# Gathers of the experts' stage without a bounds check: 80 indirect DMAs on GpSimd's queue

## The chip, the cores and the metric

One core of one Trainium2 chip runs the whole program. The metric is the device time of one execution in microseconds (us); the time before is the median of 3 runs.

## The reference, cut to what matters

8 sequences of 1024 tokens, 128 numbers each. A Mamba-2 mixer with an MLP comes first, then a mixture of experts; both with a layer norm ahead of them, a layer norm behind them, and a residual. The part around the change is the second:

```python
probs = jax.nn.softmax(x @ Wr + br, axis=-1)
gates, ids = jax.lax.top_k(probs, K)               # N = 8192 tokens, K = 2, E = 8
...
valid = rank < cap                                 # cap = ceil(1.2 * N / E) = 1229 tokens for each expert
pos = jnp.where(valid, s_ids * cap + rank, E * cap)
disp_tok = jnp.zeros((E * cap + 1,), jnp.int32).at[pos].set(s_tok)[:E * cap]
xg = x[disp_tok].reshape(E, cap, Dm)               # the gather
h = jax.nn.silu(jnp.einsum('ecd,edh->ech', xg, W1) + b1[:, None, :])
out = jnp.einsum('ech,ehd->ecd', h, W2) + b2[:, None, :]
gated = out * disp_g.reshape(E, cap, 1)
y = jnp.zeros((N, Dm), x.dtype).at[disp_tok].add(gated.reshape(E * cap, Dm))
```

## The kernel before, in words

The program has stages that end in a barrier of all engines: norms and decays, the state-space mixer, its MLP, routing, and last the experts' stage with the final sum and norm. Routing writes a table `token_rows` of 8192 rows to HBM; a row is a token's 128 numbers and its two gates, 130 float32, 520 bytes. It also leaves two arrays of row numbers in SBUF, `token_of` and `choice_of`, each 128 x 80 uint32. Each expert has a region of 1280 slots (10 columns of 128), of which 1229 can hold a token: the last column of each expert always has 51 vacant rows or more. A vacant slot's `token_of` is clamped to a row number of the table (line 1741: max with 0), and its `choice_of` is a number beyond the 16384 rows of `choice_rows`, so that the scatter leaves that row out.

The experts' stage (lines 1745 to 2022) goes over 24 blocks `n` of 2 to 4 columns: `sizes` is (2, 4, 4) for the first expert, (4, 3, 3) for the next six, (4, 4, 2) for the last. Each block passes through these steps, each on one engine:

- `fetch(n)`, GpSimd (line 1865 on; the DMA is recorded as line 1871): one indirect DMA for each column gathers 128 rows of `token_rows` into `xg`, a ring of 8 blocks. It waits for block n - 8 to have left `xg` (`need` on `s_pt`, `s_g1`, `s_g2`).
- `turn(n)`, TensorE (line 1891): transposes into `e_pT`; it waits for the gathers of its block. VectorE copies them to `e_xgT` (line 1984) and makes the gates (lines 1975 to 1980).
- `up(n)` (line 1900), `silus(n)` on ScalarE (line 1943), `down(n)` (line 1908), `outs(n)` on ScalarE (line 1950), `back(n)` (line 1916): two matmul layers and the transpose back.
- `results(n)`, VectorE (line 1992): times the gate, into `yo`, a ring of 8 blocks.
- `leave(n)`, GpSimd (line 1875 on; the DMA is recorded as line 1879): one indirect DMA for each column scatters the rows into `choice_rows`. It waits for `results(n)`.

The order on each engine is written out by `staged([(lag, step), ...])`: at turn i it issues each step for block i - lag, in the order of the list. On GpSimd that is `staged([(0, fetch), (LAG, leave)])` with LAG = 5: fetch(0) to fetch(5) come first, then leave(0), fetch(6), leave(1) and so on, and after fetch(23) and leave(18) the last five `leave` stand alone. On TensorE it is up(i - 2), down(i - 3), back(i - 4), turn(i). So of GpSimd's 160 indirect DMAs the first 20 are gathers, then the two kinds alternate in groups of 2 to 4: 19 times a scatter follows a gather, and 18 times a gather follows a scatter.

Behind the experts, SyncE waits for the last scatters (line 1851) and loads `choice_rows` in 19 groups (lines 1854, 1855); TensorE adds the two choices (line 1931), VectorE and ScalarE do the norm (lines 2000 to 2019), SyncE stores.

With `bounds_check=TOKENS - 1` each indirect DMA of line 1871 is preceded on GpSimd's queue by a register instruction (MOVE) that puts 8191 into a register, which the DMA names as an operand; line 1879 does the same with 16383.

Of the kernel before, what the change touches and what calls it, by code (L numbers as in the profile page):

```python
# [36 lines left out]
TOKENS = SEQS * LEN  # L37
# [22 lines left out]
def need(eng, sem, t, back=0):  # L60

    value = t + 1 - back
    if not isinstance(value, int) or value > 0:
        eng.wait_ge(sem, value)
# [33 lines left out]
def build(nc, x, ln_w, ln_b, in_proj_w, conv_w, conv_b, dt_bias, A_log, D_skip, rms_w, out_proj_w,  # L98
# [4 lines left out]
    with ExitStack() as ctx:  # L103
# [9 lines left out]
        def sem(name):  # L113
            s = nc.alloc_semaphore(name=name)
            stage_sems.append(s)
            return s
# [484 lines left out]
        with ExitStack() as st:  # L601
# [45 lines left out]
            def staged(stages):  # L647

                for i in range(PAIRS + max(lag for lag, _ in stages)):
                    for lag, stage in stages:  # L650
                        if 0 <= i - lag < PAIRS:
                            stage(i - lag)
# [1092 lines left out]
        with ExitStack() as st:  # L1745
# [9 lines left out]
            RING = 8  # L1755
# [59 lines left out]
            s_xg = [sem(f"e_xg{k}") for k in range(RING)]  # L1815
# [47 lines left out]
            @block.gpsimd  # L1863
            def _(g):
                def fetch(n):
                    need(g, s_pt, n, RING)
                    need(g, s_g1, n, RING)
                    need(g, s_g2, n, RING)
                    for i in range(sizes[n]):
                        c = starts[n] + i  # L1870
                        g.indirect_dma_start(xg[:, n % RING, i, :], None, table,  # L1871
                                             bass.IndirectOffsetOnAxis(ap=token_of[:, c:c + 1], axis=0),
                                             bounds_check=TOKENS - 1, oob_is_err=False).then_inc(s_xg[n % RING], 16)

                def leave(n):
                    need(g, s_yo, n)
                    for i in range(sizes[n]):
                        c = starts[n] + i
                        g.indirect_dma_start(choice, bass.IndirectOffsetOnAxis(ap=choice_of[:, c:c + 1], axis=0),  # L1879
                                             yo[:, n % RING, i, :], None, bounds_check=2 * TOKENS - 1,  # L1880
                                             oob_is_err=False).then_inc(s_scat[n % RING], 16)
                g.wait_ge(filled, 16 * FILLS)
                staged([(0, fetch), (LAG, leave)])
# [161 lines left out]
```

## Time and profile before

| | |
|---|---|
| median of 3 runs | 878.65 us (876.77 to 880.98) |
| the profiled execution | 879.82 us; its span in the profile 878.1 us |
| TensorE's mean granted clock | 0.885 of 2.4 GHz |
| experts' stage, first gather to end of last scatter | 613.6 to 831.5 us |
| engines, share of the span busy | TensorE 81%, VectorE 69%, ScalarE 56%, GpSimd 50% |

PE is TensorE's matmuls, DVE VectorE, ACT ScalarE, POOL GpSimd, SP SyncE; POOLq and SPq are what those engines' queues issue themselves. Times of rows count from the start of the span. "issue" as a releaser means that the engine waited for nothing that the profile shows. Durations of single GpSimd instructions are given in ns.

### The profile page before, as it was taken

The numbers are of one execution on the slowest core, as the hardware profiler recorded it, in microseconds if no ns is written. First come the engines' busy times: TensorE is split into PE (matmuls) and PEld (weight loads), VectorE is DVE, ScalarE is ACT, GpSimd is POOL, SyncE is SP. The second block draws the span as 40 slices with busy tenths as digits, with TensorE's granted clock in tenths as the row PEclk, the third lists the DMA queues.
The fourth block names the chain that finished last, engine by engine and source line by source line (L and its number), as shares of the span: only waits on it lengthen the run. The fifth ranks groups of instructions, "written<-read, shape, count | busy, mean of one in ns | idle before, by whom it ended". The sixth has DMA issues, their size and how long they took to land. (4 is left out here: it accounts for less than half of the span.)

```text
span 878.1 us, 14619 instructions
## 1 busy us (share of the span) xinstructions
PE 710.7 (81%) x3872; PEld 493.1 (56%) x3872; DVE 606.9 (69%) x2161; ACT 490.8 (56%) x1207; POOL 442.8 (50%) x576
## 2 busy tenths in 40 slices
PE   7657999999999997899999721046698888888994
PEld 3425677777777775798989720023354444444442
DVE  7957999999999993799999868897111211121067
ACT  4864666676667675687877415434243432334157
POOL 7612767667667664234433350000757777777500
PEclk8867999999999999999999855555699998999998
DMA  9930000000000001500000004000322212221196
GB/s 219 388 129 14 1 1 1 2 1 1 2 1 1 1 1 34 159 1 2 3 1 1 1 0 196 0 0 2 99 64 72 74 50 74 73 75 50 41 352 219
DMA packets 50414, 52.92 MB, mean 60 GB/s; under 512 B 7576, under 2 KB 39624, under 8 KB 50080
## 3 DMA queue, kind: packets, MB, share of 16 engines
q1 hardware_dynamic: 44496, 41.62, 14.6%
q0 software_dynamic: 5120, 10.37, 4.4%
q8 instruction: 30, 0.49, 0.2%
q14 instruction: 48, 0.39, 0.1%
q10 hardware_dynamic: 720, 0.05, 0.1%
HBM read 28.04 MB, written 24.18 MB: 59 GB/s over the span
## 5 line engine op out<-in xcount | busy, mean ns | idle before, releaser
L890 DVE SCALAR_TENSOR_TENSOR s_cv<-s_pU,tap_w,s_cv 128x256 f32<-128x256 f32 x372 | 153.4, 476 | 12.4 <-ACT s_cv L821 12.0
L1871 POOL DMA_INDIRECT arena<-token_rows,token_of x80 | 81.4, 1017 | 112.3 <-issue 111.7
L1992 DVE TENSOR_TENSOR arena<-e_pB,e_gate 128x384 f32<-128x384 f32 (+2 forms) x24 | 14.5, 603 | 123.9 <-PE e_pB L1916 123.9
L1879 POOL DMA_INDIRECT choice_rows<-arena,choice_of x80 | 79.7, 996 | 32.7 <-issue 22.6
L1943 ACT ACTIVATE e_h<-e_pH,e_bcols 128x384 f32<-128x384 f32 (+2 forms) x96 | 58.7, 616 | 65.6 <-PE e_pH L1900 63.1
L1900 PE MATMUL e_pH<-e_xgT,e_w 128*128 128x384 f32 (+2 forms) x192 | 83.4, 584 | 0.0
L689 POOL TENSOR_TENSOR s_xa<-s_xt,arena 128x512 f32<-128x512 f32 x32 | 34.5, 1077 | 88.3 <-ACT s_xt L839 88.3
L821 ACT ACTIVATE s_cv<-s_pU,tap_b,tap_w 128x256 f32<-128x256 f32 x124 | 63.7, 561 | 23.4 <-PE s_pU L723 23.0
L723 PE MATMUL s_pU<-arena,w_in 128*128 128x262 f32 x248 | 69.3, 403 | 7.7 <-DVE s_cv L890 3.4
L1908 PE MATMUL e_pO<-e_h,e_w 128*128 128x384 f32 (+2 forms) x192 | 72.7, 522 | 0.4 <-ACT e_oT L1950 0.4
L1372 PE MATMUL m_pM<-w_m,m_h 128*128 128x128 f32 x512 | 62.5, 275 | 0.1
L1363 PE MATMUL m_pH<-m_hT,w_m 128*128 128x256 f32 x256 | 60.7, 380 | 2.1 <-ACT m_h L1246 1.5
L1372 PEld LDWEIGHTS m_pM<-w_m,m_h 128*128 128x128 f32 x512 | 59.7, 192 | 0.3 <-issue 0.3
L1900 PEld LDWEIGHTS e_pH<-e_xgT,e_w 128*128 128x128 f32 x192 | 40.1, 220 | 28.9 <-issue 21.2
L1908 PEld LDWEIGHTS e_pO<-e_h,e_w 128*128 128x128 f32 x192 | 36.7, 191 | 33.3 <-issue 20.6
L1207 POOL TENSOR_TENSOR arena<-arena,m_un 128x256 f32<-128x256 f32 (+1 forms) x32 | 22.5, 703 | 64.9 <-DVE m_un L1282 64.9
L723 PEld LDWEIGHTS s_pU<-arena,w_in 128*128 128x128 f32 x248 | 43.0, 197 | 17.0 <-DVE s_cv L890 7.6
L1363 PEld LDWEIGHTS m_pH<-m_hT,w_m 128*128 128x128 f32 x256 | 46.2, 190 | 7.5 <-ACT m_hT L1239 2.6
L1246 ACT ACTIVATE m_h<-m_pH,b_col 128x256 f32<-128x256 f32 x128 | 50.2, 485 | 0.0
L1984 DVE COPY e_xgT<-e_pT 128x384 f32<-128x384 f32 (+2 forms) x24 | 14.4, 599 | 48.3 <-PE e_pT L1891 48.3
L1950 ACT ACTIVATE e_oT<-e_pO,e_bcols 128x384 f32<-128x384 f32 (+2 forms) x24 | 14.8, 617 | 54.8 <-PE e_pO L1908 54.8
L701 POOL TENSOR_TENSOR s_y<-s_y,s_dx 128x512 f32<-128x512 f32 x32 | 40.9, 1277 | 4.9 <-DVE s_y L923 4.9
(305 smaller groups left out, 1874.3 us busy)
## 6 DMA issues: line engine op xcount, KB each, us to landing
choice_rows<-zrow SPq DMA_DIRECT2D x16, 512.0 KB, 7.7
arena<-choice_rows SPq DMA_DIRECT2D x28, 256.0 KB, 5.3
token_rows<-arena SPq DMA_DIRECT2D x8, 520.0 KB, 5.8
n_x<-in_L_attn_x_dram SPq DMA_DIRECT2D x8, 512.0 KB, 7.6
arena<-in_L_attn_x_dram SPq DMA_DIRECT2D x8, 512.0 KB, 4.8
e_w<-in_L_ffn_W_dram SPq DMA_DIRECT2D x16, 256.0 KB, 3.2
out_dram<-arena SPq DMA_DIRECT2D x14, 256.0 KB, 4.2
decay_rows<-arena SPq DMA_DIRECT2D x2, 1024.0 KB, 4.8
```

The costliest lines, as they stand in the source:

```text
L701: g.tensor_tensor(y2[:, :], y1[:, p % 2, :], dx[:, p % 4, :], ALU.add).then_inc(s_y2, 1)
L723: pe.matmul(pU[m % 2][:, 0:G2 * XBLK], w_in[:, P * m:P * (m + 1)], xT[:, G2 * p:G2 * (p + 1), :].rearrange("p t c -> p (t c)"), start=True ...
L821: a.activation(by_tile(cv[:, p % 2, m, :]), columns(m)[:, :, 0:P], ACT.Identity, bias=tap_b[:, m:m + 1], scale=tap_w[:, m, 0:1]).then_inc( ...
L890: v.scalar_tensor_tensor(out=by_tile(cv[:, p % 2, m, :]), in0=columns(m)[:, :, tap:tap + P], scalar=tap_w[:, m, tap:tap + 1], in1=by_tile( ...
L1246: ins = a.activation(h1[:, m % NB, c, :], pH[half_][:, N * (c % 2):N * (c % 2 + 1)], ACT.Relu, bias=b1_col[:, c:c + 1])
L1363: ins = pe.matmul(pH[half_][:, N * c:N * (c + 1)], w_m1[:, P * f:P * (f + 1)], hT[:, m % NB, :], start=True, stop=True)
L1372: ins = pe.matmul(pM[m % 2][:, P * i:P * (i + 1)], h1[:, m % NB, c, P * i:P * (i + 1)], w_m2[:, c, :], start=(c == 0), stop=(c == NF - 1))
L1871: g.indirect_dma_start(xg[:, n % RING, i, :], None, table, bass.IndirectOffsetOnAxis(ap=token_of[:, c:c + 1], axis=0), bounds_check=TOKENS ...
L1879: g.indirect_dma_start(choice, bass.IndirectOffsetOnAxis(ap=choice_of[:, c:c + 1], axis=0), yo[:, n % RING, i, :], None, bounds_check=2 * ...
L1900: pe.matmul(pH[c][:, 0:w], we1[:, expert(n) % 2, P * c:P * (c + 1)], xgT[:, n % 3, 0:w], start=True, stop=True).then_inc(s_ph, 1)
L1908: ins = pe.matmul(pO[:, 0:w], we2[:, expert(n) % 2, c, :], hb[:, n % 2, c, 0:w], start=(c == 0), stop=(c == NF - 1))
L1943: a.activation(hb[:, n % 2, c, 0:w], pH[c][:, 0:w], ACT.Silu, bias=bcols[:, f:f + 1]).then_inc(s_h, 1)
```

## The change

The keyword `bounds_check` is taken away from the gathers. The scatters of line 1879 keep theirs.

```diff
@@ fetch(n)
                         c = starts[n] + i
                         g.indirect_dma_start(xg[:, n % RING, i, :], None, table,
                                              bass.IndirectOffsetOnAxis(ap=token_of[:, c:c + 1], axis=0),
-                                             bounds_check=TOKENS - 1, oob_is_err=False).then_inc(s_xg[n % RING], 16)
+                                             oob_is_err=False).then_inc(s_xg[n % RING], 16)
```

## Rows read from the trace of the kernel before

**Rows 1.** The page: span, engines' busy time, the span in 40 slices.
```profile
span 878.1 us, 14619 instructions
...
PE 710.7 (81%) x3872; PEld 493.1 (56%) x3872; DVE 606.9 (69%) x2161; ACT 490.8 (56%) x1207; POOL 442.8 (50%) x576
...
PE   7657999999999997899999721046698888888994
...
POOL 7612767667667664234433350000757777777500
PEclk8867999999999999999999855555699998999998
```

**Rows 2.** Busy time by stretches of 26 us: time, busy (instructions), clock, DMA share, GB/s.
```profile
core 0: us, PE busy (x) PEld busy (x) DVE busy (x) ACT busy (x) POOL busy (x), PEclk, DMA share, GB/s
643.00:669.50 26.50, 26.50 (x90) 14.59 (x89) 5.70 (x20) 12.79 (x20) 19.17 (x19) 1.00 0.22 64
669.50:695.50 26.00, 20.26 (x66) 11.31 (x65) 4.52 (x15) 9.12 (x15) 19.90 (x21) 0.93 0.25 71
722.00:748.00 26.00, 21.42 (x66) 12.06 (x65) 4.47 (x15) 8.39 (x14) 19.90 (x21) 0.87 0.26 70
774.00:800.00 26.00, 19.98 (x65) 11.26 (x64) 4.68 (x15) 7.75 (x14) 19.90 (x21) 0.93 0.27 71
sum 157.00, PE 132.45 PEld 73.70 DVE 28.37 ACT 57.07 POOL 119.17; mean PE 22.07 PEld 12.28 DVE 4.73 ACT 9.51 POOL 19.86
```

**Rows 3.** Waits by engine, stretch 610 to 840: total us, times, longest us.
```profile
POOL arena L1871 <- issue: 111.7, 78, 88.2
PE e_pT L1891 <- DMA arena<-token_rows,token_of: 33.1, 15, 5.3
POOL choice_rows L1879 <- issue: 22.6, 74, 0.3
POOL choice_rows L1879 <- DVE arena L1992: 10.2, 6, 5.2
POOL arena L1871 <- DVE arena L1992: 0.6, 2, 0.3
```

**Rows 4.** GpSimd in order of time (start us, us; idle before in brackets).
```profile
613.64 1.26 POOL L1871 DMA_INDIRECT arena<-token_rows,token_of  x1 [88.18 <-issue]
615.21 1.00 POOL L1871 DMA_INDIRECT arena<-token_rows,token_of  x1 [0.31 <-issue]
...
644.84 1.03 POOL L1879 DMA_INDIRECT choice_rows<-arena,choice_of  x1 [5.16 <-DVE arena L1992]
...
790.65 1.05 POOL L1871 DMA_INDIRECT arena<-token_rows,token_of  x1 [0.30 <-issue]
792.00 1.01 POOL L1871 DMA_INDIRECT arena<-token_rows,token_of  x1 [0.30 <-issue]
793.32 1.00 POOL L1871 DMA_INDIRECT arena<-token_rows,token_of  x1 [0.30 <-issue]
794.62 1.00 POOL L1871 DMA_INDIRECT arena<-token_rows,token_of  x1 [0.30 <-issue]
795.93 1.02 POOL L1879 DMA_INDIRECT choice_rows<-arena,choice_of  x1 [0.30 <-issue]
...
801.20 1.01 POOL L1871 DMA_INDIRECT arena<-token_rows,token_of  x1 [0.30 <-issue]
```

**Rows 5.** Lines 1871 and 1879, all: duration ns min/median/max, first and last start.
```profile
L1871 POOLq MOVE  x80: 29/29/29, 612.7 to 790.2; - x80
L1871 POOL DMA_INDIRECT arena<-token_rows,token_of x80: 993/1001/1258, 613.6 to 801.2; - x80
L1879 POOL DMA_INDIRECT choice_rows<-arena,choice_of x80: 978/986/1031, 644.8 to 830.5; - x80
```

**Rows 6.** Line 1871 in the stretch 616 to 618.
```profile
L1871 POOLq MOVE  x3: 29/29/29, 616.4 to 617.5; - x3
```

**Rows 7.** The chain that ended last (start us, us), three stretches.
```profile
625.63 2.85 DMA arena<-token_rows,token_of
628.53 1.12 PE e_pT L1891 x4
629.65 4.64 PE e_pH L1900 x8
...
639.89 3.43 PE e_pO L1908 x8
...
794.62 2.72 DMA arena<-token_rows,token_of
797.39 0.66 PE e_pT L1891 x4
...
817.44 0.70 DVE arena L1992
```

**Rows 8.** Line 1879, single scatters: a full column (829.2), one with vacant rows (830.5).
```profile
L1879 POOL DMA_INDIRECT choice_rows<-arena,choice_of x1: 985/985/985, 829.2 to 829.2; - x1
L1879 POOL DMA_INDIRECT choice_rows<-arena,choice_of x1: 985/985/985, 830.5 to 830.5; - x1
```

**Rows 9.** Line 1871, one gather that follows a scatter.
```profile
L1871 POOL DMA_INDIRECT arena<-token_rows,token_of x1: 1047/1047/1047, 647.5 to 647.5; - x1
```

## The prediction

> **What bounds the kernel now.** I read the page first. GpSimd (POOL) is half busy over the whole span, but seven or eight tenths busy in the slices of the experts' stage, the only stage that the change touches [rows 1]. The table by stretches says which engine sets the pace there: POOL shows 19.90 us in each, TensorE 20.0 to 21.4 in the three that stand behind the first, at a clock of 0.87 to 0.93 [rows 2]. 19.90 of 26 looks like slack. It isn't: in order of time each indirect DMA of POOL lasts about 1.00 us and is followed by 0.30 us in which POOL waits for nothing that the profile shows, over and over [rows 4]. One column costs POOL 1.30 us for its gather and about 1.29 for its scatter, so an expert of 10 columns costs 26 us whatever TensorE does. The waits agree. TensorE waits 33.1 us for gathers to land, 15 times, while POOL waits for VectorE's results only 10.8 us in all, 5.2 of them once, at 644.84 [rows 3, 4]. Between 644.84 and 795 POOL is the bound.
>
> Two stretches of the stage are different, and the chain shows both [rows 7]. At the start block 0 to 2 have to be gathered: the 10th gather is issued at 625.63, lands at 628.5, and from there to the first scatter TensorE is the chain. The other ten of the first 20 gathers fall in POOL's idle 5.16 us ahead of that scatter. At the end, from 797.39 (the landing of the gather of 794.62, the 78th) to 817.44, TensorE is again the chain, and the last two gathers, 799.85 and 801.20, lie beside it.
>
> So a nanosecond saved on each gather counts 10 + 58 = **68 times** of 80: the first ten, and numbers 21 to 78. That holds until TensorE becomes the bound: of the 157 us from 643 to 800 it is idle 157 - 132.45 = 24.6 us [rows 2], which is the most that the 58 could bring.
>
> **The change, part by part.**
>
> *The 80 MOVE instructions go.* Each lasts 29 ns [rows 5], 2.3 us together. They are on POOL's sequencer, which runs ahead of the part that builds the transfers: between 616.4 and 617.5 it issues three MOVEs, one each 0.54 us [rows 6], while a gather takes 1.30 us; the MOVE of the last gather is issued by 790.2, its DMA starts at 801.20 [rows 4, 5], some 11 us later. A shorter sequencer step gives a longer queue, not an earlier DMA. What hides it is the 0.54 against 1.30; without that cover it would be 68 x 0.029 = 2.0 us. Only the first MOVE, at 612.7 with nothing ahead of it, is on the path: 0.03 us. The waits of `fetch` on TensorE and VectorE now stand before the DMA itself instead of before its MOVE; they have cost 0.6 us in all [rows 3], and a scatter behind them would wait for a later event anyway. I take 0.
>
> *The gather's own time.* Here is the only real unknown: how much of the 1001 ns is the comparison of 128 row numbers with 8191. No row shows an unchecked gather. Below: nothing, if the routine compares whether or not it is asked to. The nearest rows are scatters with and without rows left out. The last column of an expert has 51 vacant rows of 128; its scatter took 985 ns, and the full column before it 985 ns [rows 8]. Leaving rows out costs and saves nothing, so the comparison isn't a fork with a long arm. Between the two kinds, gather and scatter, the medians differ by 1001 - 986 = 15 ns [rows 5], and that is the size of a small difference in the work for each row. I take that 15 ns: 68 x 0.015 = 1.0 us. The upper end is a comparison that is a full step of the work on each row. 1001 / 128 = 7.8 ns for each row; reading the number, comparing, forming the address, writing the source's entry, writing the destination's, stepping on are six steps, and one in six of 1001 is 167 ns, an estimate from the row and my count of steps: 68 x 0.167 = 11.3 us. A loss is not excluded either (rival B).
>
> *What comes earlier.* With a gather of 986 ns instead of 1001 an expert takes 25.85 us of POOL, TensorE waits a little less, and its clock may stay up a little more. The transfers are the same in size and number, so nothing lands later. Scatters follow their gathers' pace. Behind the experts the last scatters, the loads and the norm move as a block.
>
> **The sum**: 879.82 - 0.03 - 1.0 = 878.8 us against the profiled execution. That execution was 1.2 us above the median of the runs, 878.65, so against the median 877.6 us. This kernel's runs spread over 4.2 us; what can be told from no change is 0.5%, 4.4 us, or 65 ns on each gather by the 68.
>
> **Rival A, faster by a percent: the comparison is work on each row, one row after the other.** For it: the gather is POOL's bound and takes 1 us for 128 rows [rows 5], which looks like a loop. Against it: 51 rows left out changed nothing [rows 8]. Price: 167 ns a gather, 878.65 - 11.3 = 867.3 us. The GPSIMD Engine Reference of the Trainium skill (section 3.1, Elementwise) gives about 12 cycles an element to branching that depends on data. The table of datapath clocks in the skill's Advanced Engine Details and Errata has this engine at 1.2 GHz; with 128 rows one after the other this would be 1.28 us, an estimate, more than the whole row, and with 64 on each of two cores 0.64 us. By that figure the 58 gathers would run into TensorE's 24.6 us and the ten first ones give 6.4, 847.6 us. The trace speaks against it by the equal 985 ns. I give the rival 0.25, of which that extreme is 0.02.
>
> **Rival B, slower: an unchecked gather is another routine than a checked scatter, and each change of kind is paid cold.** Place: the 37 changes of kind on POOL's queue, about 36 of them in the stretch that POOL bounds. For it: changes already cost something. A gather behind a scatter takes 1047 ns [rows 9] where most take 1001, 46 more, and the very first took 1258, 257 more [rows 5]. If each change cost what the first start cost, 257 - 46 = 211 ns more than now, that is 36 x 0.21 = 7.6 us: 886.3 us. It decides from 4.4 / 36 = 122 ns a change. Against it: a checked gather and a checked scatter are two kinds already, and they cost 46 ns a change. Chance 0.11.
>
> **Rival C, the change doesn't do what it says:** without the keyword the bound is filled in from the table's size, MOVEs and all. Then nothing moves, 878.65. Nothing in the rows of before speaks to it. Chance 0.10.
>
> **How the numbers follow.** My case, a gather shorter by 0 to 60 ns, has 0.54; its own range with the runs' spread is 873.5 to 880.5 us. A has 0.25, B 0.11, C 0.10. Faster by over 0.5% is A: 0.25. Within 0.5% are my case and C: 0.64. Slower is B: 0.11. The range reaches from A's price to halfway towards B's, 867 to 882 us: it leaves out B and the stronger third of A, just under 0.2.
>
> **What would show it.** The MOVEs of line 1871 gone and 14619 - 80 = 14539 instructions; if they are there, it is C. The gather's median near 986 ns with 0.30 us behind it: my case; near 830: A. The scatter that follows a gather still at 1.02 us and the gather behind a scatter 0.05 above the others: no B; both near 1.2: B. The first scatter should start 10 times, the 78th gather 68 times the saving earlier than at 644.84 and 794.62, and the end of the span should follow the 78th one to one. I am wrong in the pass-through if the gathers get shorter and POOL waits for VectorE by as much more, and wrong in the cover if the gathers keep 1001 ns and the 0.30 us behind them shrinks by 29 ns: then the MOVE was on the path, and it is 2.0 us.

## The result, and the profile after

The changed kernel takes 875.51 us, the median of 8 runs (874.1 to 876.41), against 878.5 us for the kernel before in as many; the ratio is 0.9961 with a 95% interval of 0.9949 to 0.9973, some 3.4 us (the two medians differ by 3.0). The profiled execution took 875.28 us, its span is 873.6. This is a gain, and one that lies inside the 0.5% that the prediction called no change.

The page of the changed kernel, lines that answer to [rows 1]:

```profile
span 873.6 us, 14539 instructions
...
PE 708.7 (81%) x3872; PEld 491.5 (56%) x3872; DVE 607.3 (70%) x2161; ACT 490.1 (56%) x1207; POOL 438.0 (50%) x576
```

80 instructions are gone, the MOVEs, and POOL is busy 4.8 us less; TensorE, VectorE and ScalarE have the same instructions. Line 1871 and line 1879 of the changed kernel, the answer to [rows 5] (duration in ns, minimum/median/maximum):

```profile
L1871 POOL DMA_INDIRECT arena<-token_rows,token_of x80: 940/947/1192, 612.5 to 796.7; - x80
...
L1879 POOLq MOVE  x80: 29/29/29, 642.7 to 819.0; - x80
L1879 POOL DMA_INDIRECT choice_rows<-arena,choice_of x80: 980/984/1023, 643.5 to 825.9; - x80
```

The gather fell from 1001 to 947 ns, its minimum from 993 to 940 and the first one from 1258 to 1192. The scatters, which keep their check, stand where they stood (984 ns, before 986). GpSimd in order of time, the answer to [rows 4]:

```profile
612.51 1.19 POOL L1871 DMA_INDIRECT arena<-token_rows,token_of  x1 [88.15 <-issue]
614.01 0.96 POOL L1871 DMA_INDIRECT arena<-token_rows,token_of  x1 [0.30 <-issue]
...
624.01 0.95 POOL L1871 DMA_INDIRECT arena<-token_rows,token_of  x1 [0.30 <-issue]
...
643.46 1.02 POOL L1879 DMA_INDIRECT choice_rows<-arena,choice_of  x1 [6.03 <-DVE arena L1992]
...
790.28 0.94 POOL L1871 DMA_INDIRECT arena<-token_rows,token_of  x1 [0.30 <-issue]
791.53 1.02 POOL L1879 DMA_INDIRECT choice_rows<-arena,choice_of  x1 [0.31 <-issue]
...
825.93 0.98 POOL L1879 DMA_INDIRECT choice_rows<-arena,choice_of  x1 [0.30 <-issue]
```

The 0.30 us between instructions hasn't changed. With the same five points of both kernels the 4.5 us between the two spans can be laid out (us; the last scatter of before started at 830.49):

| from ... to | before | after | difference |
|---|---|---|---|
| start of the span, first gather | 613.64 | 612.51 | -1.13 |
| first gather, 10th gather | 11.99 | 11.50 | -0.49 |
| 10th gather, first scatter | 19.21 | 19.45 | +0.24 |
| first scatter, 78th gather | 149.78 | 146.82 | -2.96 |
| 78th gather, last scatter | 35.87 | 35.65 | -0.22 |
| last scatter, end | 47.61 | 47.67 | +0.06 |

The first line is hardly the change's: the last VectorE instruction ahead of the first gather starts 1.05 us earlier already, and in the twelve other profiled executions of this study the first gather starts anywhere from 611.8 to 614.8. Only 0.08 us is left for the missing MOVE: the first gather starts 2.13 us behind the start of that VectorE instruction where it was 2.21. The other lines add up to -3.4 us, about the measured gain. That they agree so well is partly chance, since between the executions of this study the third line moves from 16.9 to 19.5 us, the fifth from 35.2 to 37.4 and the last from 46.3 to 48.5. The second and the fourth line repeat: in every execution with such gathers unchecked they are 11.48 to 11.51 and, with checked scatters, 146.82 to 146.86. The first ten gathers brought nine times 54 ns, the 57 from the first scatter to the 78th gather brought 57 x 52 ns.

The +0.24 of this execution is TensorE's clock. The chain of the changed kernel behind the 10th gather, the answer to the first stretch of [rows 7]:

```profile
624.01 2.79 DMA arena<-token_rows,token_of
626.80 0.04 issue
626.84 1.12 PE e_pT L1891 x4
627.96 4.95 PE e_pH L1900 x8
632.91 1.73 PE e_pO L1908 x8
```

TensorE starts 1.7 us earlier than before, but the eight matmuls that took 4.64 us take 4.95. The table by stretches of the changed kernel (PE, PEld, DVE, ACT, POOL busy, then the granted clock) shows why: the clock goes from 1.2 to 2.4 GHz in the slice from 630 to 631.

```profile
629.00:630.00 1.00, 1.00 (x2) 0.34 (x1) 0.10 (x1) 0.29 (x1) 0.94 (x1) 0.50 0.27 67
630.00:631.00 1.00, 1.00 (x2) 0.34 (x1) 0.00 (x0) 0.39 (x1) 0.75 (x1) 0.56 0.26 71
631.00:632.00 1.00, 1.00 (x4) 0.50 (x3) 0.00 (x0) 0.69 (x1) 0.69 (x2) 1.00 0.19 50
```

More of the work that now begins earlier is done at the lower clock. This isn't a fixed price of the change: in other executions with these gathers unchecked the stretch took 17.5 or 19.2 us (see the last section). The waits of POOL for results, 10.8 us before [rows 3], are 11.6 us:

```profile
PE e_pT L1891 <- DMA arena<-token_rows,token_of: 29.3, 14, 5.5
POOL choice_rows L1879 <- issue: 22.1, 72, 0.5
POOL choice_rows L1879 <- DVE arena L1992: 11.6, 8, 6.0
```

6.0 of them is the pause before the first scatter, 5.2 before. The ten gathers behind the tenth end earlier, and their gain goes into that pause, as it should. TensorE waits 29.3 us for gathers instead of 33.1.

The 0.5 us that is now the longest under "issue" is also a wait for results. It stands ahead of the third scatter:

```profile
649.83 0.69 DVE L1992 TENSOR_TENSOR arena<-e_pB,e_gate 128x512 f32<-128x512 f32 x1 [6.34 <-PE e_pB L1916]
...
651.34 1.02 POOL L1879 DMA_INDIRECT choice_rows<-arena,choice_of  x1 [0.49 <-issue]
```

The scatter starts 0.82 us behind the end of the results, as the first scatter does (0.85). Before, the four gathers ahead of it took longer and it found the results ready, with a pause of 0.30. So these four gathers, numbers 21 to 24, gave back 0.19 us, nearly all that they had saved. So the stretch lost 2.96 us, and 2.7 to 3.1 against the other executions with the check, where 57 x 54 ns would be 3.1.

### The profile page after: what moved, and what is told of

Read it like the earlier page. It is cut to its first block and busy times, and to the rows that moved or that the text cites. A ratio compares the mean times of both kernels' runs of the same rounds, so it can differ in the third digit from the quotient of the medians.

```text
span 873.6 us, 14539 instructions
## 1 busy us (share of the span) xinstructions
PE 708.7 (81%) x3872; PEld 491.5 (56%) x3872; DVE 607.3 (70%) x2161; ACT 490.1 (56%) x1207; POOL 438.0 (50%) x576
## 3 DMA queue, kind: packets, MB, share of 16 engines
q0 software_dynamic: 5120, 10.37, 4.3%
## 5 line engine op out<-in xcount | busy, mean ns | idle before, releaser
L1871 POOL DMA_INDIRECT arena<-token_rows,token_of x80 | 77.0, 963 | 112.2 <-issue 112.2
L1908 PEld LDWEIGHTS e_pO<-e_h,e_w 128*128 128x128 f32 x192 | 36.5, 191 | 33.1 <-issue 20.5
L723 PEld LDWEIGHTS s_pU<-arena,w_in 128*128 128x128 f32 x248 | 42.5, 194 | 16.9 <-DVE s_cv L890 7.7
```

Source lines behind the costliest of these rows:

```text
L723: pe.matmul(pU[m % 2][:, 0:G2 * XBLK], w_in[:, P * m:P * (m + 1)], xT[:, G2 * p:G2 * (p + 1), :].rearrange("p t c -> p (t c)"), start=True ...
L1871: g.indirect_dma_start(xg[:, n % RING, i, :], None, table, bass.IndirectOffsetOnAxis(ap=token_of[:, c:c + 1], axis=0), oob_is_err=False).t ...
L1908: ins = pe.matmul(pO[:, 0:w], we2[:, expert(n) % 2, c, :], hb[:, n % 2, c, 0:w], start=(c == 0), stop=(c == NF - 1))
```

## The experiments

The theory to test: the 54 ns are the check inside the gather's own instruction, the MOVE costs nothing, and 68 of the 80 gathers count.

### One register for all: is it the MOVE?

```diff
+                limit = nc.alloc_register(g.engine, name="limit")
+                g.reg_mov(limit, TOKENS - 1)
 ...
-                                             bounds_check=TOKENS - 1, oob_is_err=False)
+                                             bounds_check=limit, oob_is_err=False)
```

> The gathers keep their bounds check, but 8191 is put into one register once, so 79 of the 80 MOVEs of line 1871 are gone. Theory (the time is in the comparison inside the gather's own instruction; the MOVE is covered by the queue): gathers keep a median of about 1001 ns, the end stays within 1 us of before, ratio 0.999 to 1.001. Rival (the MOVE, or the register that it has just written, is what the gather waited for): gathers near 947 ns and a ratio near 0.996.

Measured: 879.03 us, ratio 0.9992 (0.9974 to 1.001). One MOVE is left where there were 80, and the gathers are as long as before (first the line of the one MOVE, then that of the gathers):

```profile
L1866 POOLq MOVE  x1: 29/29/29, 610.8 to 610.8; - x1
```
```profile
L1874 POOL DMA_INDIRECT arena<-token_rows,token_of x80: 992/1000/1257, 611.8 to 797.4; - x80
```

The interval alone would leave room for the 2.0 us that uncovered MOVEs would cost. The trace doesn't: from the first scatter to the 78th gather it takes 149.58 us, and four executions with all the MOVEs of those gathers took 149.56 to 149.91; 57 MOVEs on the path would be 1.65 us. The 0.30 us between instructions didn't shrink either. So the gathers' MOVEs were worth nothing that can be measured, and the check was worth the 54 ns. (The profiled execution ended 3.2 us earlier than that of the kernel before, not within the 1 us that was expected; it gained 1.9 us ahead of the first gather, 1.7 between the 10th gather and the first scatter and 0.6 behind the last scatter, and lost 1.2 behind the 78th gather, stretches that vary whatever the kernel.)

### The MOVE without the check

```diff
+                        g.reg_mov(limit, TOKENS - 1)
                         g.indirect_dma_start(xg[:, n % RING, i, :], None, table,
 ...
-                                             bounds_check=TOKENS - 1, oob_is_err=False)
+                                             oob_is_err=False)
```

> The gathers are unchecked, but a MOVE of 8191 into a register stands ahead of each, as before; nothing reads it. Theory: gathers 947 ns, ratio near 0.996, the same as the change itself. Rival (the MOVE is what cost): gathers near 1001 ns or gaps of 0.33 us instead of 0.30 between them, ratio 0.999 to 1.001.

This experiment tested nothing. Its page shows that the MOVEs, which nothing read, had been dropped from the program, since it has as many instructions as the changed kernel:

```profile
span 871.3 us, 14539 instructions
```

It is the changed kernel once more: 875.14 us, ratio 0.9952 (0.9934 to 0.997). The changed kernel itself, run beside it:

> The changed kernel as it is, beside the others on the same chip: ratio 0.996, gathers 947 ns.

875.19 us, ratio 0.9953 (0.9937 to 0.997), gathers 947 ns. By their ratios the three measurements of this program have 3.4, 4.2 and 4.1 us, by their medians 3.0 to 3.3.

### Which gathers count

Only the first 20 gathers unchecked (`bounds_check=TOKENS - 1 if n > 5 else None`):

> Only the first 20 gathers (blocks 0 to 5) are unchecked. Theory: 10 of them count, 10 x 56 ns = 0.56 us, ratio 0.9985 to 1.0; the time from the first scatter's start to the last one's stays at 185.65 us. Rival (they all count, or an earlier start is multiplied): ratio below 0.998.

878.45 us, ratio 1.0001 (0.9989 to 1.0014). The ratio is a hair above the range that was expected, and its interval holds both 0.56 us and nothing. The time between first and last scatter was 831.17 - 643.82 = 187.35 us and not 185.65; 1.57 of the 1.7 us are behind the 78th gather, and the section on the hardware comes back to it. From the first scatter to the 78th gather it was 149.91 us against 149.78, so the early gain didn't multiply. From the first gather to the 10th it took 11.49 us instead of 11.99, so the first ten do bring their half microsecond. That the other ten bring nothing is seen from the 10th gather to the first scatter, among executions in which the clock behaved alike: 17.47 to 17.52 us in three with these gathers unchecked, 17.54 and 17.57 in two with the check, where ten times 54 ns would be 0.54.

Only the other 60 unchecked (`if n < 6 else None`):

> Only the other 60 gathers (blocks 6 to 23) are unchecked. Theory: 58 of them count one to one, 58 x 54 ns = 3.1 us; ratio about 0.9965, and the time from the first scatter's start to the last one's shrinks from 185.65 us to 182.5. Rival (TensorE or the waits for results give part back): it shrinks by less than 2.5 us.

875.94 us, ratio 0.9967 (0.9955 to 0.9979). The first scatter is at 645.47, the 78th gather at 792.30, the last scatter at 828.01: 146.83 us, as in the changed kernel, and 182.54 us, as expected. These 60 gathers carry most of the gain, nearly one to one: all that comes back is the 0.19 us ahead of the third scatter, which is there too.

### Per row or per instruction

Both kernels of this pair fetch 64 rows with each gather instead of 128 and leave the other half of the tile as it was; one keeps the check, one drops it.

```diff
-                        g.indirect_dma_start(xg[:, n % RING, i, :], None, table,
-                                             bass.IndirectOffsetOnAxis(ap=token_of[:, c:c + 1], axis=0),
+                        g.indirect_dma_start(xg[0:P // 2, n % RING, i, :], None, table,
+                                             bass.IndirectOffsetOnAxis(ap=token_of[0:P // 2, c:c + 1], axis=0),
```

> Each gather fetches 64 rows instead of 128 (partitions 0 to 63; the rest of the tile keeps what it held), with the bounds check. To be read against e6_half_rows_unchecked by the gathers' medians. Theory (the comparison is made once for each row number): the checked gather of 64 rows is 27 ns longer than the unchecked one. Rival (a fixed price of the instruction's form, for example reading the bound's register): 54 ns longer, as with 128 rows.

> The same with 64 rows and no bounds check. Theory: 27 ns below e5_half_rows_checked. Rival: 54 ns below it.

The first 20 gathers, which have no scatter between them, with the check and then without:

```profile
L1871 POOL DMA_INDIRECT arena<-token_rows,token_of x20: 938/942/1197, 612.6 to 636.5; - x20
```
```profile
L1871 POOL DMA_INDIRECT arena<-token_rows,token_of x20: 899/903/1144, 612.4 to 635.6; - x20
```

And the same 20 gathers of 128 rows, before and after:

```profile
L1871 POOL DMA_INDIRECT arena<-token_rows,token_of x20: 993/1000/1258, 613.6 to 638.7; - x20
```
```profile
L1871 POOL DMA_INDIRECT arena<-token_rows,token_of x20: 940/944/1192, 612.5 to 636.5; - x20
```

The check costs 56 ns with 128 rows and 39 ns with 64. Neither side had it right: that is 22 ns for the instruction and 0.27 ns a row, if the price is a straight line, which two points can't show. The more useful reading is the other difference. 64 rows fewer save 58 ns with the check and 41 ns without: 0.9 and 0.6 ns a row. On a straight line, which is again an estimate, some 880 of a gather's 1000 ns don't depend on how many rows it has; what was measured is that 942 of them are there with half of the rows. Single times of the two kernels, 872.17 us each, don't rank them; both are of one execution.

### Direction or length of the row

The gathers read the input `x`, whose rows are 512 bytes, with the same row numbers, with and without the check; the gates in the tile stay as they were.

```diff
-                        g.indirect_dma_start(xg[:, n % RING, i, :], None, table,
+                        g.indirect_dma_start(xg[:, n % RING, i, 0:D], None, x.rearrange("b l d -> (b l) d"),
```

> The gathers read 512-byte rows of the input x (same row numbers, 128 float32) instead of the 520-byte rows of the table, with the check; the gates in the tile are left as they were. A scatter has rows of 512 bytes too, and there the check costs 12 to 16 ns, not 54. If the row's length is what makes the difference, the checked and the unchecked gather differ by 12 to 16 ns here; if it is the direction (the indexed side is the source), by about 54 ns as before.

> The same with 512-byte rows and no bounds check: 12 to 16 ns below e8_plain_rows_checked if the row's length makes the price, about 54 ns below if the direction does.

Checked, then unchecked, all 80:

```profile
L1871 POOL DMA_INDIRECT arena<-in_L_attn_x_dram,token_of x80: 992/999/1257, 612.6 to 799.9; - x80
```
```profile
L1871 POOL DMA_INDIRECT arena<-in_L_attn_x_dram,token_of x80: 940/948/1192, 612.4 to 796.4; - x80
```

51 ns, so the row's length is not what makes a gather's check dearer than a scatter's. What does, beside the direction, stays open.

### Half of the rows left out

```diff
-                                             bounds_check=TOKENS - 1, oob_is_err=False)
+                                             bounds_check=TOKENS // 2 - 1, oob_is_err=False)
```

> The bound of the gathers is 4095 instead of 8191, so about half of the rows are left out and keep what the tile held. My argument was that the comparison is no fork with a long arm, since a scatter with 51 rows left out took as long as a full one. If that holds for gathers: median 1001 ns, as before. If a row left out takes another path: the median moves by more than 20 ns either way.

```profile
L1871 POOL DMA_INDIRECT arena<-token_rows,token_of x80: 992/1000/1257, 612.4 to 798.1; - x80
```

1000 ns where it was 1001. The rows were left out indeed: GpSimd's DMA queue moved 7.85 MB instead of 10.37, and the missing 2.5 MB are 47% of what the gathers fetch. Whether a row number lies within the bound or beyond it makes no difference to the time; only whether there is a bound does.

### The scatters too

If a check costs GpSimd time, the other 80 are next. A scatter needs its check to leave vacant slots out, so these now get a row of their own behind the 16384, which nobody reads.

```diff
-    choice = nc.dram_tensor("choice_rows", (2 * TOKENS, D), F32, kind="Internal").ap()
+    choice = nc.dram_tensor("choice_rows", (2 * TOKENS + SLOTS, D), F32, kind="Internal").ap()
 ...
+                g.iota(spare[:, :], [[P, COLS]], base=2 * TOKENS + 1, channel_multiplier=1, allow_small_or_imprecise_dtypes=True)
 ...
-                link(v.tensor_scalar(vacant[:, :], acc[:, 0, :], 0.0, FAR, ALU.is_equal, ALU.mult))
+                link(v.scalar_tensor_tensor(out=vacant[:, :], in0=acc[:, 0, :], scalar=0.0, in1=spare[:, :],
+                                            op0=ALU.is_equal, op1=ALU.mult))
 ...
-                                             yo[:, n % RING, i, :], None, bounds_check=2 * TOKENS - 1,
+                                             yo[:, n % RING, i, :], None,
```

> Beside the gathers, the 80 scatters are unchecked as well; vacant slots now write to spare rows behind the 16384 of choice_rows instead of being left out. Theory: the comparison costs a scatter about as much as a gather, 985 to about 930 ns; 60 scatters lie ahead of the 78th gather on the stretch that GpSimd bounds and 10 behind TensorE's chain at the end, so 70 x 0.054 = 3.8 us beside the change's 3.4, some 871.5 us, ratio 0.992. Rival 1 (the cost is special to gathers): scatters 985 ns, ratio 0.996. Rival 2 (TensorE is now the bound, or the 408 spare rows cost transfers): scatters shorter, but GpSimd's waits for VectorE grow from 12 us by as much, ratio 0.995 or more.

870.74 us, ratio 0.9906 (0.9877 to 0.9934), and the scatters are shorter by much less than expected. The last 17 and 14 of them, with the check (changed kernel) and without:

```profile
L1879 POOL DMA_INDIRECT choice_rows<-arena,choice_of x17: 980/982/985, 801.9 to 825.9; - x17
```
```profile
L1882 POOL DMA_INDIRECT choice_rows<-arena,choice_of x14: 963/969/972, 801.5 to 821.4; - x14
```

13 ns, not 54: the time came out as forecast while its reason had failed. So it was run again.

> e3_scatters_too once more. By its scatters (median 969 to 972 instead of 982 to 984 ns, 12 to 15 ns each) 70 of them are worth 0.8 to 1.1 us beside the change's 3.4: ratio 0.9945 to 0.996. The first measurement had 0.9906 [0.9877, 0.9934], 3 us more than that. If this repeats, something beside the scatters' own time is gained; if the ratio is near 0.995, the first was a lucky draw.

871.49 us, ratio 0.992 (0.9901 to 0.9939). It repeated: by both ratios the kernel is 0.8 to 0.9% faster than the one before. Beside the changed kernel on the same chip (0.9937 to 0.997, the first measurement) it is faster too, by intervals that just don't touch. In the stretch from the first scatter to the 78th gather, which the clock hardly moves, it takes 786.18 - 640.43 = 145.75 us and 788.60 - 642.88 = 145.72 us against 146.82: 1.1 us, 19 ns for each of 57 scatters (the expectation counted 60). The ten last scatters at 13 ns add 0.1.

Another 1.0 us lies ahead of scatters, where the text above saw no price. A checked scatter has its MOVE behind the wait for the results. While the queue is full that is hidden; where GpSimd has run out of work and waits, it isn't. This is the chain near the end, in the changed kernel and then with unchecked scatters:

```profile
812.89 0.70 DVE arena L1992
813.59 0.02 issue
813.61 0.03 POOLq L1879
813.64 0.49 issue
814.13 0.03 POOLq L1879
814.16 0.19 issue
814.35 0.32 POOL choice_rows L1879
```
```profile
808.93 0.70 DVE arena L1995
809.63 0.27 issue
809.90 0.97 POOL choice_rows L1882
```

From the end of the results to the start of the scatter it is 0.76 us with the check and 0.27 without. At the first scatter it is 0.84 to 0.85 us in all twelve executions with checked scatters and 0.29 in both without. These two places bring 0.55 and 0.49 us. (The third scatter waits for results too, and keeps the first of the two: it starts 0.28 us behind them instead of 0.82.) The MOVE and the check went together here, so that it is the MOVE is read off the chain and not tested alone.

By the ratios on that one chip the kernel leads the changed one by 4.1 us, by the second measurement by 2.9; 2.2 are now accounted for. The runs fall into two groups, eight of twelve in 870.3 to 870.8 and three in 874.3 to 875.0, and the two profiled ones are one of each, 870.72 and 874.35. Between those two the first gather differs by 0.5 us, the stretch from the 10th gather to the first scatter by 1.9 and the one behind the 78th gather by 1.5. The latter two are TensorE's clock, see below. Whether this kernel really meets the good case more often, and why, is open.

## Why the prediction was right, and where its reason was off

**The bound** was read rightly: POOL's 1.30 us a column. The 57 gathers between the first scatter and the 78th gather returned 52 ns each, and the 60-only experiment returned the same. One reading was loose: POOL does not show 19.90 us in each stretch of [rows 2] but 19.17 in the first, where TensorE is busy for all 26.50. There the two engines are nearly level, and that is where four gathers gave back 0.19 us.

**The 68.** Right within a few: 68 x 0.054 = 3.67 us by this count, and 3.43 by the lines of the table between the first gather and the last scatter. In that one execution the start gave back 0.24 us to the clock and the end added 0.22 to the gain. The first ten gathers are shorter by their 0.49 us in the trace, which is too little for the runs' times to tell.

**The MOVEs at nothing.** Right for these 80, shown by the one register: 79 of 80 gone, and the stretch of 57 gathers as long as before. The cover was the one named, a sequencer ahead of its engine, and it holds only while the queue has work: at the first gather the MOVE cost 0.08 us and not 0.03, and at a scatter that waits for results about 0.5 us. No gather of this kernel waits with an empty queue but the first.

**The gather's own time** is the term that was mis-sized. I took 15 ns from [rows 5], where the gather measured 54. The step that failed was to read the difference between a checked gather and a checked scatter as the size of a small difference in the work on each row: both rows contain the check, so their difference says nothing of it. What the 54 ns are inside the instruction is not split further: 17 of them go with the second 64 rows, and the rest needn't be a comparison of rows at all. The bounds, 0 and 167 ns, held it, and so did the 0 to 60 ns that the prediction gave its own case, though it didn't say where the 60 came from. The sum would have been 878.65 - 3.7 = 875.0 us with 54 ns, and 875.51 was measured.

**The argument against a fork** [rows 8] held: half of all rows left out, and the same 1000 ns. But it bounds the difference between the two outcomes of a comparison, not the comparison. That is why it was right against rival A and no help for the size.

**Rival A** is refuted with its picture of a loop of 7.8 ns a row: between 64 and 128 rows a row costs 0.6 to 0.9 ns, and 0.27 of that is the check. The rule that the Trainium skill gives in the GPSIMD Engine Reference (section 3.1, Elementwise), some 12 cycles an element for branching that depends on data, doesn't describe this instruction: the measured increment is 0.27 ns a row between 64 and 128 rows.

**Rival B** is refuted. A gather behind a scatter takes 0.99 us, 40 ns more than the other gathers' mean, where it was 46 [rows 9], and the scatter behind a gather still takes 1.02. **Rival C** is refuted by the missing MOVEs.

**The range** was wide for what was known. That the gain stayed inside the 0.5%, as forecast, has luck in it: with 65 ns on the gather, 9 more than the first twenty showed, it would have been the 4.4 us that the prediction left to rival A, and the intervals of all three measurements reach beyond 0.5%. The line itself was drawn too wide: an interval of 0.9949 to 0.9973 tells 3.4 us from nothing.

## What to carry to other kernels

Where GpSimd issues indirect DMAs back to back, count columns times 1.3 us before looking at anything else. A bounds check on a gather of 128 rows costs it some 54 ns, on a scatter some 13 to 20. The register instruction ahead of it costs nothing while the queue is full, and some 0.5 us where GpSimd has been waiting for the data: look there first. Fewer instructions should matter more than cheaper ones, since 94% of a gather's time is there with half of its rows; no run here tried fewer. A price is found by a row that lacks the thing beside one that has it: two rows that both have it, however close, don't bound it.

## What the runs showed of the hardware that was not expected

TensorE's clock can move this kernel's time by as much as the change does. At the start of the experts' stage the clock rises from 1.2 to 2.4 GHz at a time that differs between executions, of one program too: in the slice from 631 to 632 before, 6 us behind the 10th gather, and from 627 to 628 in the second run of the changed kernel, 2 us behind it:

```profile
627.00:628.00 1.00, 0.76 (x2) 0.04 (x1) 0.00 (x0) 0.98 (x4) 0.84 (x1) 0.56 0.35 67
628.00:629.00 1.00, 0.52 (x5) 0.52 (x6) 0.00 (x0) 0.27 (x1) 0.86 (x1) 1.00 0.30 67
```

There the 10th gather and the first scatter are 17.47 us apart, where before they were 19.21 and in the first run of the changed kernel 19.45. All 14 profiled executions fall into these two cases: the six in which the clock is at 1.2 GHz for 6 us behind the 10th gather took 18.9 to 19.5 us, the eight in which it had risen within 4 us took 16.9 to 17.6. The changed kernel met the long case in its first profiled execution and the short one in its two others.

Near the end there is a second such place. While POOL is the bound TensorE pauses, and now and then the clock falls for some microseconds. Ahead of the 78th gather it costs nothing that shows: that stretch took 146.82 to 146.86 us in five executions with unchecked gathers and checked scatters. If it falls behind the 78th gather it lies on the chain. With one register for all, and in the changed kernel:

```profile
792.00:797.00 5.00, 3.56 (x8) 2.09 (x9) 1.00 (x4) 0.64 (x1) 3.94 (x4) 0.66 0.17 48
```
```profile
792.00:797.00 5.00, 4.16 (x13) 2.21 (x14) 1.55 (x5) 2.09 (x4) 3.78 (x5) 1.00 0.14 43
```

The first has 0.66 and needs 37.07 us from the 78th gather to the last scatter; the second has 1.00 and needs 35.65. In the 4 us ahead of that window TensorE was busy for 2.50 us in the first and for 3.77 in the second. Here too all 14 executions fit: the five with some 3.4 us at 1.2 GHz, beginning 2 to 3 us behind the 78th gather, took 36.7 to 37.4 us, the nine others 35.2 to 35.9. The 1.7 us by which the first-20 experiment missed its expected 185.65 us are nearly all this: its last stretch took 37.44 us.

A saving of 50 ns on an instruction also moves what else happens when, and may move which of these cases is met. Of the five executions whose gathers from the 21st on are checked (all 128 rows, checked scatters) three met the long case at the end; of the five with them unchecked none did. That hints at it and is too few to show it.
